# Differential cross attention and ternary FFN on one core: scores ahead of gelu's sums, h_hi ahead of two q_hi, and a prologue with seven staging tiles, other value buffers and four banks of row scores

## The reference, cut to what matters

```python
# x (4, 2048, 512), ctx (4, 154, 512), all float32
x = x + attention(layernorm(x), ctx)
x = x + ffn(x)

def attention(q, ctx):             # 16 heads of 32, 8 key heads, each used twice
    q1, q2 = split(q @ Wq.T)       # Wq 1024 x 512
    k1, k2 = split(ctx @ Wk.T)     # Wk  512 x 512
    v = ctx @ Wv.T                 # Wv  256 x 512
    w = softmax(q1 @ k1.T) - lam * softmax(q2 @ k2.T)
    a = w @ v
    a = a * rsqrt(mean(a * a) + 1e-5) * g * (1 - LAMBDA_INIT)
    return a @ Wo.T

def ffn(x):
    h = layer_norm(x, ln1_g, ln1_b)
    h = gelu(h @ ternary(w1).T + b1)          # w1 2048 x 512, exact gelu
    h = layer_norm(h, ln2_g, ln2_b)           # over the 2048 hidden units
    return h @ ternary(w2).T + b2             # w2 512 x 2048
```

## Time and profile before

| | us |
|---|---|
| median of 3 runs | 2291.74 (2291.2 to 2291.82) |
| the profiled execution | 2290.26 |
| its span, first to last instruction | 2288.5 |
| around the span | 1.76 |
| PE busy | 2139.8 (94%) |
| DVE busy | 1783.9 (78%) |
| ACT busy | 1516.7 (66%) |
| POOL busy | 1066.2 (47%) |
| DMA queue of SP, share of 16 engines | 25.4% |
| PE's granted clock, mean over the span | 0.962 |

### The profile page before, as it was taken

The page is one execution under the profiler, slowest core; times in us unless marked ns, Lnnn a source line. Parts: engine busy times, 40 slices in busy tenths (PEclk is TensorE's granted clock), DMA queues, the critical chain, the costliest instruction groups (busy, mean ns, idle before and its releaser), DMA issues.

```text
span 2288.5 us, 45380 instructions
## 1 busy us (share of the span) xinstructions
PE 2139.8 (94%) x18239; PEld 1184.0 (52%) x18239; DVE 1783.9 (78%) x2700; ACT 1516.7 (66%) x1973; POOL 1066.2 (47%) x803
## 2 busy tenths in 40 slices
PE   7777999999999999999999999999999999999988
PEld 5444555554555555455555555555555555555443
DVE  3678878787987968788787878888786888878773
ACT  3467676766667676666767666676766667675754
POOL 2312726436272643627264363726436372643526
PEclk9869999999999999999999999999999999999999
DMA  7414122130423213031331303132150323212020
GB/s 291 125 46 95 44 80 70 34 97 23 117 48 84 65 35 101 22 98 48 87 78 40 103 16 97 48 93 56 44 118 13 98 46 94 56 46 68 2 57 19
DMA packets 253009, 160.16 MB, mean 70 GB/s; under 512 B 171812, under 2 KB 221580, under 8 KB 252288
## 3 DMA queue, kind: packets, MB, share of 16 engines
q1 hardware_dynamic: 249792, 152.07, 25.4%
q0 software_dynamic: 3008, 5.20, 0.8%
HBM read 51.82 MB, written 20.38 MB: 32 GB/s over the span
## 4 chain that ended last, share of the span: by engine, by line
PE 67%; DVE 16%; ACT 7%; issue 4%; POOL 3%; DMA 2%; SPq 0%; POOLq 0%; ACTq 0%; DVEq 0%
PE ps L1608 17%; PE ps L1626 11%; PE ps L1511 5%; PE ps L1636 5%; PE ps L1458 4%; PE ps L1543 4%; PE ps L1460 4%; PE ps L1459 4%; DVE attn_raw L1155 2%; PE ps L1572 2%; ACT arena L873 2%; PE ps L1573 2%; POOL attn_raw L687 2%; PE ps L1571 2%; DVE arena L1125 2%
## 5 line engine op out<-in xcount | busy, mean ns | idle before, releaser
L687 POOL TENSOR_TENSOR attn_raw<-attn_raw 128x512 f32<-128x512 f32 x448 | 629.4, 1424 | 48.1 <-ACT attn_raw L844 21.9
L1608 PE MATMUL ps<-rows,w1T 128*128 128x512 f16 x2048 | 483.9, 379 | 22.8 <-DVE rows L1246 22.8
L1125 DVE TENSOR_REDUCE arena<-ps 128x6 f32<-128x924 f32 (+1 forms) x330 | 349.3, 1083 | 41.5 <-PE ps L1511 40.9
L663 POOL TENSOR_TENSOR q<-q 128x512 f16<-128x512 f32 x128 | 190.5, 1492 | 333.5 <-ACT q L803 332.5
L1251 DVE SCALAR_TENSOR_TENSOR arena<-attn_raw,vec_cols,arena 128x512 f16<-128x512 f32 x256 | 299.3, 1173 | 34.2 <-ACT arena L842 34.1
L1626 PE MATMUL ps<-w2T,arena 128*128 128x512 f16 x1440 | 325.9, 379 | 0.0
L1608 PEld LDWEIGHTS ps<-rows,w1T 128*128 128x128 f16 x2048 | 193.3, 97 | 242.6 <-DVE rows L1246 35.2
L839 ACT ACTIVATE attn_raw<-ps,vec_cols,wstep 128x512 f32<-128x512 f32 x256 | 198.9, 777 | 180.0 <-PE ps L1608 177.3
L674 POOL TENSOR_TENSOR arena<-arena,out_const 128x512 f32<-128x512 f32 x64 | 102.0, 1605 | 458.1 <-DVE arena L1287 457.0
L1155 DVE TENSOR_TENSOR attn_raw<-arena,attn_raw 128x1024 f16<-128x1024 f32 (+1 forms) x128 | 193.7, 1544 | 84.9 <-ACT attn_raw L819 82.7
L1458 PE MATMUL ps<-arena,wqT_hi 128*128 128x512 f16 x512 | 208.2, 407 | 31.6 <-ACT arena L814 25.0
(11 more groups left out here) (192 smaller groups left out, 4410.4 us busy)
## 6 DMA issues: line engine op xcount, KB each, us to landing
stack_raw<-q SPq DMA_DIRECT2D x744, 64.0 KB, 2.0
arena<-in_x SPq DMA_DIRECT2D x64, 256.0 KB, 2.9
out<-arena SPq DMA_DIRECT2D x64, 256.0 KB, 2.0
arena<-in_x SPq DMA_DIRECT2D x14, 1024.0 KB, 5.5
arena<-in_L_ffn_w SPq DMA_DIRECT2D x7, 1024.0 KB, 13.8
rows<-in_x SPq DMA_DIRECT2D x2, 1024.0 KB, 6.8
stack_raw<-in_L_xattn_Wq SPq DMA_DIRECT2D x8, 256.0 KB, 9.6
k_att<-k_store SPq DMA_DIRECT2D x4, 495.0 KB
```

The lines of the kernel that those rows point to most:

```text
L687: ins = pool.tensor_tensor(acc[:, e, :], acc[:, e, :], src[:, j % NG, :], ALU.add)
L1125: dve.tensor_reduce(negmax[:, tt:tt + 2, u0:u1], ps[:, bank:bank + 2, 0:(u1 - u0) * S].rearrange("p b (u s) -> p b u s", s=S), AX.X, ALU.m ...
L1608: ins = pe.matmul(ps[:, B_H + j % 2, :], w1T[:, k, j * P:(j + 1) * P], rows16[:, e, k, :], start=(k == 0 and e == 0), stop=(k == KD - 1 an ...
```

## The change

Four parts, called A to D here.

**A.** In ATTEND the token s0 stands ahead of g. Only PE's order changes: the first scores of a block are issued ahead of gelu's sums of the block before. (On ACT and DVE only one of the two tokens issues anything.)

**B.** In ATTEND t2 stands ahead of v6. Only DVE's order changes: the two attn_lo of t2 ahead of the six instructions of normalise(6).

**C.** ACT issues h_hi (block i) ahead of q_hi of the next block's query tile 6 (QEARLY - 1), where it stood behind it; PE's order is the same.

**D.** The prologue. Seven staging buffers, the two new ones the halves of q32; ACT doesn't wait for the constants ahead of the first tile's copy; the pieces v_new for batches 2 and 3 lie in p16_raw and q16, so that all four are set to zero at the start and v_second with its wait is gone; in their place ACT's q_hi(0, 2) waits for the value store of batch 3 and the first exponentials for that of batch 2. Row scores of block 0 take four banks and are reduced two tiles at a time (L1125's form, 22 reductions instead of 44). The ternary tiles take two banks instead of four.

```diff
 ATTEND = [(w[0], int(w[1:] or 0)) for w in (
-    "c e1 k14 k15 e2 g y0 y1 s0 l0 q0 s1 l1 q1 s2 v0 l2 h1 s3 v1 l3 h2 t0 y2 z0 z1 s4 v2 l4 q2 z2 s5 v3 l5 q3 t1 s6 v4 l6 h3 "
-    "s7 v5 l7 h4 v6 t2 y3 z3 v7").split()]
+    "c e1 k14 k15 e2 s0 g y0 y1 l0 q0 s1 l1 q1 s2 v0 l2 h1 s3 v1 l3 h2 t0 y2 z0 z1 s4 v2 l4 q2 z2 s5 v3 l5 q3 t1 s6 v4 l6 h3 "
+    "s7 v5 l7 h4 t2 v6 y3 z3 v7").split()]
...
+        NROW = 4
         def row_bank(c, tb):
-            return (B_O, B_L, 0, 1)[tb % row_banks(c)]
-        def row_banks(c):
-            return 4 if c else 2
+            return (B_O, B_L, 0, 1)[tb % NROW] if c else (B_O, B_L, 1, 2)[tb % NROW]
...
-        NSTG = 5
-        stage = stack_raw[:, o2:o2 + NSTG * D].rearrange("p (n d) -> p n d", n=NSTG)
+        NSTG = 7
+        stage = [stack_raw[:, o2 + n * D:o2 + n * D + D] for n in range(5)]
...
+        stage += [q32[:, n, :] for n in range(2)]
...
-        v_new = [attn_raw[:, at:at + 3 * TB // 2] for at in (6 * TB, 15 * TB // 2, 0, 3 * TB // 2)]
-        v_first, v_second = attn_raw[:, 6 * TB:], attn_raw[:, 0:3 * TB]
+        v_new = [attn_raw[:, at:at + 3 * TB // 2] for at in (6 * TB, 15 * TB // 2)]
+        v_new += [p16_raw[:, 2 * TB:7 * TB // 2], q16[:, 1].rearrange("p a b t -> p (a b t)").bitcast(F32)[:, 0:3 * TB // 2]]
...
-        TERN_BANK = (0, 1, 2, 4)
+        TERN_BANK = (0, 4)
...
             def setup():
-                act.wait_ge(s_consts, 1)
...
                         act.wait_ge(s_kv, len(KGRP) + b + 1)
-                        act.wait_ge(s_v0, 1 + b // 2)
...
+                if c == 0 and n == 2:
+                    act.wait_ge(s_vst[3], 16)
...
+                elif c == 0:
+                    act.wait_ge(s_vst[2], 16)
...
                 if ahead:
-                    for n in range(QATT, QEARLY):
+                    for n in range(QATT, QEARLY - 1):
                         q_hi(i + 1, n)
                 h_hi(i)
                 if ahead:
-                    for n in range(QEARLY, QM):
+                    for n in range(QEARLY - 1, QM):
                         q_hi(i + 1, n)
...
-                dve.memset(v_first, 0.0).then_inc(s_v0, 1)
+                for b in range(BATCH):
+                    ins = dve.memset(v_new[b][:, VM:], 0.0)
+                ins.then_inc(s_v0, 1)
...
-                        if b == 2:
-                            dve.wait_ge(s_kst, 16 * 3 * KUNITS // UPT)
-                            dve.memset(v_second, 0.0).then_inc(s_v0, 1)
...
             def row_maxima(c, tbs):
-                if c == 0:
-                    for tb in tbs:
-                        row_max(c, tb)
-                else:
-                    for tb in tbs[::2]:
-                        row_max_pair(c, tb)
+                for tb in tbs[::2]:
+                    row_max_pair(c, tb)
...
             def ternary(n):
                 pe.wait_ge(s_sign, n + 1)
-                if n >= 4:
-                    pe.wait_ge(s_ternC, n - 3)
+                if n >= 2:
+                    pe.wait_ge(s_ternC, n - 1)
                 else:
-                    pe.wait_ge(s_xt_lo, min(n + 1, TT - 1))
+                    pe.wait_ge(s_xt_lo, 1)
...
-                if tb >= row_banks(c):
-                    wait(pe, s_tmax, c, NT, tb - row_banks(c) + (2 - tb % 2 if c else 1))
-                elif tb == 2:
+                if tb >= NROW:
+                    wait(pe, s_tmax, c, NT, tb - NROW + 2 - tb % 2)
+                elif tb == 2 and c:
                     wait(pe, s_q32, c, QM, QM)
```

More of the change, by code:

```diff
@@ L401, in ternary_bank @@
         def ternary_bank(n):
-            return TERN_BANK[n % 4]
+            return TERN_BANK[n % 2]
         def ternary_out(n):
@@ L453, in setup @@
                         sp.wait_ge(s_tile, n - NSTG + 1)
-                    sp.dma_start(stage[0:rows, n % NSTG, :], src).then_inc(s_stage[n % NSTG], 16)
+                    sp.dma_start(stage[n % NSTG][0:rows, :], src).then_inc(s_stage[n % NSTG], 16)
                     if n == VEC_AT:
@@ L853, in ternary_sign @@
                     act.wait_ge(s_vst[n // 7], 16)
-                elif n == 8:
-                    act.wait_ge(s_vst[2], 16)
-                    act.wait_ge(s_vst[3], 16)
                 elif n >= JH + 2:
@@ L1110, in x_rows_lo @@
                                       ALU.subtract).then_inc(s_xr_lo, 1)
-            def row_max(c, tb):
-                b, tt = divmod(tb, TT)
-                u0, u1 = UPB * b, min(UPB * b + UPB, UNITS)
-                wait(dve, s_t, c, NT, tb + 1)
-                dve.tensor_reduce(negmax[:, tt, u0:u1],
-                                  ps[:, row_bank(c, tb), 0:(u1 - u0) * S].rearrange("p (u s) -> p u s", s=S),
-                                  AX.X, ALU.max, negate=True).then_inc(s_tmax, 1)
             def row_max_pair(c, tb):
@@ L1343, in _ @@
                 elif what == "m":
-                    for tt in range(TT):
-                        if n == 0 and tt == 0:
-                            dve.wait_ge(s_sign, 1)
-                        row_max(0, n * TT + tt)
+                    if n == 0:
+                        dve.wait_ge(s_sign, 1)
+                    row_maxima(0, range(n * TT, n * TT + TT))
                 elif what == "n":
@@ L1369, in setup @@
                     for k in range(KD):
-                        ins = pe.transpose(ps[:, n % 4, k * P:k * P + rows], stage[0:rows, n % NSTG, k * P:(k + 1) * P],
+                        ins = pe.transpose(ps[:, n % 4, k * P:k * P + rows], stage[n % NSTG][0:rows, k * P:(k + 1) * P],
                                            ident[0:rows, 0:rows])
```

## The result

The changed kernel takes 2213.7 us (median of 4 runs, 2212.03 to 2218.68), the kernel before 2291.78 (4 runs, 2291.2 to 2291.82). The ratio is 0.9663, 95% interval 0.9647 to 0.968: by the ratio 77 us less. The forecast was 2217 with a range of 2200 to 2246. The profiled execution took 2212.26 us, with a span of 2210.4, 78.1 less than before.

A forecast was written before the change was run, and what follows sets the result against it. PE, busy 94% of the span, was taken as the bound. A -38.7, C -18.2, B -1 and D -17 sum to -74.9 against 2290.26: 2215.4, and 2217 since the runs' median lies 1.5 higher; range 2200 to 2246.

The forecast's parts named there:

- the clock would stay up: Block boundaries, behind the sums: PE keeps full clock at most of them, so q0 ends at 424.3, not 428.47.
- thirteen other boundaries: Block boundaries before the change: thirteen more look like the one shown, with q0 at half clock taking 5.05 us.
- The 1.39 us: First hidden tile of a block: PE's wait for DVE's low part of h goes when h_hi is issued earlier.
- Block 0's 2.6: First hidden tile of block 0: 2.6 us saved by C, its wait of 2.8 being the longest.
- (1): Setup: no ACT wait for constants and two more staging buffers save 5.8 us, taken between 3.97 and 8.7.
- (2): Setup: smaller memsets at the start end PE's wait for the low part queued behind DVE's memset; 4.4 us.
- (3): Block 0's row scores: four banks and paired reductions remove waits inside steps; 6.5 us, between 0 and 7.8.
- The half clock stays: Block boundaries: the clock still falls, leaving 0.9 us gained at each; A -11.3, total 2244; chance 14%.
- The 2 us charged for that: Block boundaries: allowance of 2 us in all within A for a few where the clock still drops.
- Given back later in the block: Rest of each block, DVE at 81%: half of A and C lost, +28, 2245; chance 9%.
- DMA engines as the bound: Setup: loads from more buffers only queue; D gives -11 instead of -17, total 2223; chance 17%.
- Slower: Block boundaries: half clock grows, with a second stretch at s1; +47, 2338; chance 3%.

The follow-up runs named there:

- two banks: The changed kernel with block 0's row scores in two banks and one reduction per tile again: 2218.98 us, ratio 0.9688 to the kernel before.
- the last block's order: The changed kernel without B, with the sums ahead of s0 again in the last block alone: 2213.22 us, ratio 0.9656 to the kernel before.
- e3: The changed kernel without B, with four of sixteen w2 products moved behind the sums, ahead of y and q0: 2210.33 us, ratio 0.9642 to the kernel before.

## Why the prediction was right, step by step

**A: -38.7 forecast, 42 measured alone.** Each link was there: s0 without a wait for its stack, ACT done with its banks 3.00 us behind its start (394.75 + 1.44), the sums as cover, q0 at 2.4 GHz 3.14 us behind s0, s1 7.07 us behind the w2 products (7.0 by the sum of the prediction), with a wait of 1.18 for y1 (1.2). That the clock would stay up was a judgement there, not a sum, and the doubled sums show that it leaned too much on the standing: the clock falls without any. One reading was not exact: of the thirteen other boundaries said to look like the one shown, the first has only 3.4 us of half clock, and s1 starts 9.1 us behind its w2 products and not 10.0. Missed were two sizes. The half clock of before reached into s1, which makes steady blocks 3.4 us shorter and not 3.0. And the last block loses 4.0 us, not 1.3. Of these 4.0 the order explains some 1.0: without B, with the same order, the same wait and the same half clock at the boundary, the loss is 1.0. The other 3.0 are the later stretch of 10.2 us at half clock instead of 3.4. A alone, with 10.2 us at the boundary and 10.2 later, loses 2.7. Why the later stretch has one length or the other stays open; with the sums doubled, and B in place, it was 3.4 too.

**C: -18.2 forecast, 15 measured on top of the rest.** The 1.39 us went; 0.3 us (0.8 for 0.51) came back at the row scores where 0.2 were put. Block 0's 2.6 were a little low: from the turned maxima to the end of its w2 products the traces with C take 148.5 to 150.4 us and those without it 152.3 to 153.2. C alone gave 28 us, far more than the sum, since the boundary's clock changed with it; that the sum fits what C is worth in the whole change rests on A's having taken that half clock away.

**B: -1.** Not seen: 0.01 us in a block without half clock. The prediction found little waiting of this kind in the kernel; the 15.1 us for the attention's DMA transposes were of this kind, and B's order did not shorten them (16.6 with it, 14.3 without).

**D: -17 forecast; 18.9 us at the turned maxima of the two profiles.** (1) was 6.8 us for 5.8; (1) and (2) together 12.1 (76.07 to 63.96) for 10.2; (3), the stage of row scores, went from 58.3 to 51.6 us, 6.8 for 6.5. But these are two executions. The eight profiled with the new prologue turned the maxima at 115.5 to 118.6 us (median 118.0), the four with the old one at 134.2 to 136.7 (median 135.1): 17 us, the forecast. The new waits for the value stores cost nothing, as said: the stores had landed by 61.1 us, and q_hi(0, 2) begins at 77.5.

**The sum.** Setup and block 0 gave 21.9 us (forecast 17 + 2.6), the blocks 60.2 (42 + 15.6 - 2 + 1 = 56.6), the last one -4.0 (-1.3): 78.1 for 74.9. The error of 3 us is the half clock in s1 and 2.3 us of setup and block 0, less the last block's 2.7. That the total comes so near is in part luck: the run without B has the same program up to the first boundary and came there 2 us later, and the last block varied by 3.

**The rivals.** *The half clock stays*: A alone shows it gone at 13 of 14 boundaries. In the changed kernel and the runs with the same order and nothing else altered at the boundary it came back at 1 to 7 of 14, but only for 3.4 us, and such a block is 0.35 us longer, since s1's wait takes in the rest. The 2 us charged for that were about right. *Given back later in the block*: DVE is at 81% as that rival had it, but apart from s1's forecast wait only that of the row scores grew, by 0.3 us per block. *DMA engines as the bound*: the run with five staging tiles speaks against it, and the stores and loads kept the same full share of 1.04. The rule of the Trainium skill ("Trainium Kernel Development and Optimization", Key Constraints) that all queues share the same 16 DMA engines is not contradicted; the gain lay ahead of the full stretch. *Slower*: its mechanism, more half clock where a pause grows, was seen in the last block alone (13.6 us for 10.2), and there it cost next to nothing, as the run without B shows; A alone had the same pause and 10.2.

## What to carry to other kernels

Where an engine's clock falls behind a stretch of little work, the idle time in the list of waits is only part of the price: here 1.79 us of waiting cost 3.0 to 3.4 us. Putting real work ahead of tiny matmuls, so that they cover another engine's latency, wins both parts. Gains that two parts draw from the same slow stretch don't add: sum them by blocks in which the clock is the same, and measure one on top of the other. And a stage's gain read from two profiles can be off by the 2 to 3 us by which executions of the same program differed here: take it from as many traces as there are.

## What the runs showed that was not expected

Blocks that are all the same don't get the same clock. With C alone the half clock lasted 3.4 us at eight boundaries and 6.8 at six, with the same instructions and waits; with the sums doubled it was seven and seven.

In D alone a chance delay shows how it goes. Four boundaries in a row had 6.8 us of half clock, with blocks of 133.0 us between them. Then PE waited 2.05 us for a DMA transpose, that block took 135.58 us, and the next three boundaries had 3.4 us, none and 3.4, before it was 6.8 again. The wait, and windows at the last boundary ahead of it and at the next two behind it:

```profile
993.38 0.39 PE L1441 MATMUL ps<-woT_hi,rows 128*128 128x512 f16 x1 [2.05 <-DMA rows<-attn_raw]
935.90:942.70 6.80, 5.89 (x14) 2.05 (x15) 4.55 (x6) 3.65 (x4) 0.00 (x0) 0.50 0.00 0
1072.50:1075.80 3.30, 3.30 (x9) 1.07 (x8) 3.02 (x3) 2.05 (x2) 0.00 (x0) 0.50 0.00 0
1202.50:1208.00 5.50, 3.71 (x24) 1.54 (x20) 4.36 (x6) 4.84 (x6) 0.80 (x1) 1.00 0.01 3
```

So the moment at which a boundary comes has a part in its clock. The Trainium skill ("TensorE: Matmul & The Clock Gate", Part 1: The HAM clock gate) says that the window in which TensorE's activity is watched runs freely and isn't reset when a kernel starts. By that rule a boundary's half clock would depend on the moment at which it comes, and a change of a block's length would move it; C alone and D alone, which changed nothing at the boundary and yet its clock, agree, and so does the delayed block.

That raises a rival to the account of A: is it the order, or only the other moments that shorter blocks bring? Counted over the profiles, the first fourteen boundaries of the kernel before, C alone and D alone (the old order) had half clock at 40 of 42, 28 times for 6.8 us. Those of the changed kernel, of it without B, without C, with two banks, with five staging tiles, with the last block's order, and of A alone (the new order) had it at 28 of 98 (2, 5, 1, 6, 7, 6 and 1 of 14), never for over 3.4 us. Their blocks differ in length (129.65 us in A alone, 128.3 to 129.2 in most others), so it is the order that makes the difference, and the moment decides which of the boundaries still fall.

The clock also makes small differences hard to measure: within one comparison the kernel before lay between 2288.3 and 2294.4 us, and the versions without B, with the last block's order or with e3 can't be told apart for certain.

Six w2 products behind the sums, full-width work close to the pause, brought the half clock to ten boundaries instead of one to seven, so "more work nearby" alone doesn't predict it. The wait of 0.56 us that then stands ahead of s0 does not explain it by itself: it stood there at three of the four boundaries without half clock, too. What does was not tried.
